# Four graph-attention layers in one program: the two dot-product layers take the weighted sums of two units together

## The reference

```python
h = jnp.maximum(_layernorm(x, axis=-1), 0.0)          # before each layer
# layer 0, one head; layer 1 the same with 4 heads, biases and a leaky relu on the scores
Q = jnp.matmul(x, W_q); K = jnp.matmul(x, W_k); V = jnp.matmul(x, W_v)
scores = jnp.einsum('bnd,bmd->bnm', Q, K) * scale
scores = jnp.where(adj == 0, NEG, scores)
attn = jax.nn.softmax(scores, axis=-1)
out = jnp.matmul(attn, V)
# layer 1: out = leaky_relu(mean over the 4 heads of prop_h @ v_h, 0.2)
```

## Time and profile before

| | us |
|---|---|
| median of 3 runs (lowest, highest) | 3523.88 (3518.64, 3524.6) |
| the profiled execution, its own time | 3535.45 |
| its span, first to last instruction | 3533.6 |
| first dot layer | about 30 to 255 |
| second dot layer | about 296 to 1232 |
| additive layer, not touched | 1232 to 3178 |
| last layer, not touched | 3178 to 3533 |

### The profile page before, as it was taken

How to read it: one execution, slowest core, us unless ns; L and a number is a source line. 1 busy time by engine, 2 the same in 40 slices (tenths; PEclk the granted TensorE clock), 3 DMA queues, 4 the chain that set the end, 5 groups by cost and what they waited for, 6 DMA issues and landing times. The chain is left out here.

```text
span 3533.6 us, 78782 instructions
## 1 busy us (share of the span) xinstructions
PE 3074.6 (87%) x30972; PEld 1704.5 (48%) x30972; DVE 3034.8 (86%) x4698; ACT 2898.4 (82%) x3774; POOL 992.2 (28%) x869
## 2 busy tenths in 40 slices
PE   7988998999999879898898998988988888878875
PEld 5765666666666633333343333333333333336664
DVE  7886887878888789999999999999999999965775
ACT  4546887778877769999999999999999999975665
POOL 4434666666666600000000000000000000005674
PEclk9998999999999989999999999999999999987897
DMA  7640000000000000000000000000000000002221
GB/s 246 222 139 16 20 21 20 23 18 24 21 21 19 13 11 10 10 10 10 10 10 10 10 10 10 10 10 10 10 10 10 10 10 10 10 5 67 57 63 30
DMA packets 68411, 111.58 MB, mean 32 GB/s; under 512 B 26452, under 2 KB 26582, under 8 KB 68054
## 3 DMA queue, kind: packets, MB, share of 16 engines
q1 hardware_dynamic: 68054, 106.69, 9.8%
HBM read 86.61 MB, written 18.87 MB: 30 GB/s over the span
## 5 line engine op out<-in xcount | busy, mean ns | idle before, releaser
L1120 ACT ACTIVATE l_scalar_ring<-l_w,l_r 128x1024 f32<-128x1024 f32 x1568 | 1650.0, 1148 | 34.4 <-DVE l_values L1171 27.7
L1236 DVE TENSOR_SCALAR l_vector_ring<-l_w_code,l_r_code 128x2048 f32<-128x2048 f32 x1264 | 1605.9, 1341 | 3.1 <-PE scores L1045 0.5
L1035 PE MATMUL scores<-l_scalar_ring,l_signs 128*32 128x512 f32 x6272 | 767.9, 608 | 130.2 <-ACT l_scalar_ring L1120 129.9
L1045 PE MATMUL scores<-l_vector_ring,l_signs_code 128*32 128x512 f16 x10112 | 685.0, 396 | 90.4 <-DVE l_vector_ring L1236 89.6
L462 POOL TENSOR_TENSOR l_masked<-l_relu,mask 128x512 f32<-128x512 f32 x512 | 585.9, 1166 | 344.2 <-ACT l_relu L664 322.9
L250 ACT COPY probs_t<-turned 128x512 f32<-128x512 f32 x576 | 324.7, 587 | 430.1 <-PE turned L209 429.7
L172 POOL TENSOR_TENSOR stat<-stat,minus_half 128x8 f32<-128x8 f32 x32 | 71.6, 2239 | 1931.1 <-DVE stat L167 1931.0
L1045 PEld LDWEIGHTS scores<-l_vector_ring,l_signs_code 128*32 128x32 bf16 x10112 | 257.9, 96 | 543.2 <-DVE l_vector_ring L1236 213.8
L209 PE MATMUL turned<-ident,l_probs 128*128 128x128 f32 x3072 | 438.1, 288 | 12.2 <-issue 7.6
L277 ACT ACTIVATE l_probs<-l_logits,negmax 128x1024 f32<-128x1024 f32 x384 | 442.9, 1153 | 7.0 <-DVE negmax L268 7.0
L1035 PEld LDWEIGHTS scores<-l_scalar_ring,l_signs 128*32 128x32 f32 x6272 | 192.2, 110 | 492.3 <-issue 255.9
(11 more groups left out here) (249 smaller groups left out, 2857.6 us busy)
## 6 DMA issues: line engine op xcount, KB each, us to landing
mask<-masks_kept SPq DMA_DIRECT2D x192, 256.0 KB, 2.7
l_adj<-adj SPq DMA_DIRECT2D x64, 512.0 KB, 5.9
masks_kept<-l_mask_ring SPq DMA_DIRECT2D x64, 256.0 KB, 4.9
x_res<-x SPq DMA_DIRECT2D x8, 256.0 KB, 4.8
out<-x_res SPq DMA_DIRECT2D x8, 256.0 KB, 2.9
l_h<-l_h SPq DMA_DIRECT2D x8, 128.0 KB, 2.8
l_kl<-l_dh SPq DMA_DIRECT2D x32, 2.0 KB, 1.9
l_kl<-l_dl SPq DMA_DIRECT2D x32, 2.0 KB, 1.8
```

Of the source, the lines that this page charges most:

```text
L1035: last = nc.tensor.matmul(s.scores[g * ROWS:(g + 1) * ROWS, buf, half, :], signs[:, window], scalar_ring[:, at % SCALAR_RING, g, halves[ha ...
L1045: last = nc.tensor.matmul(s.scores[g * ROWS:(g + 1) * ROWS, buf, half, :], signs_code[:, par, g % 2, window], parts(vector_ring[:, at % VE ...
L1120: last = nc.scalar.activation(scalar_ring[:, at % SCALAR_RING, g, :], w[:, par, :], ACT.Relu, bias=r[:, par, column:column + 1])
L1236: last = nc.vector.tensor_scalar(vector_ring[:, at % VECTOR_RING, g:g + 2, :], w_code[:, par, :, :], r_code[:, par, 0, column:column + 1], ...
```

## The change

Units are taken in pairs (2p, 2p+1). The turned probabilities of a unit go to one of four buffers `probs_t[:, n % 4]`. The product of pair p runs one pair later, half of it in iteration 2p+2 and half in 2p+3: each step has four blocks of 128, and for each the two units side by side, one in either half of `outT`. There is then one `copy_out` a pair and one turn of the output a pair (`turn_pair`, 128 columns against the weights `wv_pairs`, which hold the value weights of the two heads on their diagonal), two iterations after the product began. DVE does `copy_out` at the head of the even iteration, ahead of its half copy, and finishes both units of the pair behind that copy (`finish_pair`). The pipeline runs over the end of a graph without emptying. The first two graphs are written out ahead of the loop, so that the loop runs two times in place of three.

```diff
+            def turn_pair(q, p):
+                pe.wait_ge(sems["out_copied"], STARTS + q + 1)
+                wait(pe, sems["unit_done"], STARTS + 2 * q)
+                nc.tensor.matmul(pair_out, s.turned_out[:], wv_pairs[:, p % PAIRED, :], start=True, stop=True
+                                 ).then_inc(sems["out_turned"], 1)
+
+            def pair_times_values(par, q, p, step):
+                if step == 0:
+                    pe.wait_ge(sems["half0_copied"], STARTS + 2 * q + 2)
+                    pe.wait_ge(sems["half1_copied"], STARTS + 2 * q + 2)
+                    wait(pe, sems["out_copied"], STARTS + q)
+                    wait(pe, sems["unit_done"], STARTS + 2 * q)
+                for j in range(step * NB // 2, (step + 1) * NB // 2):
+                    for odd in range(2):
+                        last = nc.tensor.matmul(s.outT[odd * D:(odd + 1) * D, 0:P], values[:, par, j, :],
+                                                probs_t[:, p % 2 * 2 + odd, j, :], start=(j == 0), stop=(j == NB - 1),
+                                                skip_group_check=True)
+                if step == 1:
+                    last.then_inc(sems["out_ready"], 1)
...
                     turn_probs(pe, s, sems, probs[:, n % 2, :], u)
-                    if n > 0:
-                        turn_out(pe, s, sems, u - 1, 0, unit_out, weights=wv[:, (n - 1) % H, :])
+                    if n % 2 == 0 and not (first and p < 2):
+                        turn_pair(b * Q + p - 2, (p - 2) % Q)
...
-                    wait(pe, sems["unit_done"], STARTS + u)
-                    if n == 0:
+                    if n == 2:
                         pe.wait_ge(sems["values_ready"], b + 1)
-                    probs_times_values(pe, s, sems, values[:, par, :, :], u)
-                turn_out(pe, s, sems, b * U + U - 1, 0, unit_out, weights=wv[:, H - 1, :])
+                    if not (first and p < 1):
+                        pair_times_values(par if p else 1 - par, b * Q + p - 1, (p - 1) % Q, n % 2)
...
+            def finish_pair(b, p):
+                v.drain()
+                finish(b, 2 * p, b * U + 2 * p)
+                if leaky:
+                    v.drain()
+                finish(b, 2 * p + 1, b * U + 2 * p + 1)
...
-                    v.drain()
-                    copy_half(v, nc.vector.tensor_copy, s, sems, 0, u)
-                    if n > 0:
-                        finish(b, n - 1, u - 1)
+                    p = n // 2
+                    if n % 2 == 0 and not (first and p < 2):
+                        copy_out(v, s, sems, b * Q + p - 2)
+                    copy_half(v, nc.vector.tensor_copy, s, sems, 0, u, probs_t[:, n % 4, :, :])
+                    if n % 2 == 0 and not (first and p < 2):
+                        if p < 2:
+                            finish_pair(b - 1, p - 2 + Q)
+                        else:
+                            finish_pair(b, p - 2)
...
-                    copy_out(v, s, sems, u)
                     for k in fills_at(n, project):
                         take_fill(b + 1, 1 - par, k)
...
-            with v.Fori(0, B // 2 - 1) as t:
-                for par in range(2):
-                    graph(2 * t + par, par, True, False)
+            graph(0, 0, True, False, first=True)
+            graph(1, 1, True, False)
+            with v.Fori(0, (B - 4) // 2) as t:
+                for i in (2, 3):
+                    graph(2 * t + i, i % 2, True, False)
```

More of the change, by code:

```diff
@@ L243, in turn_out, with copy_half @@
                        start=True, stop=True).then_inc(sems["out_turned"], 1)
-def copy_half(eng, copy, s, sems, half, u):
+def copy_half(eng, copy, s, sems, half, u, to=None):
     eng.wait_ge(sems["turned_ready"], STARTS + u + 1)
     n = s.NB // 2
-    copy(s.probs_t[:, half * n:(half + 1) * n, :], s.turned[:, half * n:(half + 1) * n, :]
+    copy((s.probs_t if to is None else to)[:, half * n:(half + 1) * n, :], s.turned[:, half * n:(half + 1) * n, :]
          ).then_inc(sems[f"half{half}_copied"], 1)
@@ L321, in dot_layer @@
     CONST = float(D)
+    PAIRED = max(1, H // 2)
+    Q = U // 2
     with ExitStack() as ctx:
@@ L332, in dot_layer @@
         wT = sb("wT", [P, 2, H, R], F32)
+        wv_pairs = sb("wv_pairs", [P, PAIRED, P], F32)
+        probs_t = sb("probs_t", [P, 4, NB, P], F32)
+        rinv = sb("rinv", [P, 8], F32)
         bias_prod = sb("bias_prod", [P, H], F32)
@@ L636, in _ @@
                 score(0, 0, u, u)
-            with pe.Fori(0, B // 2 - 1) as t:
-                for par in range(2):
-                    graph(2 * t + par, par, True, False)
+            graph(0, 0, True, False, first=True)
+            graph(1, 1, True, False)
+            with pe.Fori(0, (B - 4) // 2) as t:
+                for i in (2, 3):
+                    graph(2 * t + i, i % 2, True, False)
             graph(B - 2, 0, True, False)
             graph(B - 1, 1, False, True)
+            turn_pair(B * Q - 2, Q - 2)
+            for step in range(2):
+                pair_times_values(1, B * Q - 1, Q - 1, step)
+            turn_pair(B * Q - 1, Q - 1)
         @block.scalar
@@ L669, in graph @@
                     u = b * U + n
-                    copy_half(a, nc.scalar.copy, s, sems, 1, u)
+                    copy_half(a, nc.scalar.copy, s, sems, 1, u, probs_t[:, n % 4, :, :])
                     if not (last_graph and n + 1 == U):
@@ L766, in finish @@
                 if h == 0:
[L767 removed]
+                    nc.vector.scalar_tensor_tensor(out=acc[:], in0=unit_out[:, 0:D], scalar=scale,
                                                    in1=v_bias[:], op0=ALU.mult, op1=ALU.add).then_inc(sems["unit_done"], 1)
                 else:
[L770 removed]
+                    nc.vector.scalar_tensor_tensor(out=acc[:], in0=unit_out[:, 0:D], scalar=scale,
                                                    in1=acc[:], op0=ALU.mult, op1=ALU.add).then_inc(sems["unit_done"], 1)
@@ L776, in finish, with graph @@
                     nc.vector.scalar_tensor_tensor(out=xb, in0=leaked[:], scalar=1.0 / H, in1=xb, op0=ALU.mult, op1=ALU.add)
-            def graph(b, par, project, last_graph):
+            def finish_pair(b, p):
[4 more added lines that the diff above has]
+                finish(b, 2 * p + 1, b * U + 2 * p + 1)
+            def graph(b, par, project, last_graph, first=False):
                 for n in range(U):
                     u = b * U + n
-                    v.drain()
-                    copy_half(v, nc.vector.tensor_copy, s, sems, 0, u)
-                    if n > 0:
-                        finish(b, n - 1, u - 1)
+                    p = n // 2
+                    if n % 2 == 0 and not (first and p < 2):
[6 more added lines that the diff above has]
+                            finish_pair(b, p - 2)
                     if not last_graph or n + 2 < U:
@@ L800, in graph @@
                         take_values(b + 1, 1 - par)
-                v.drain()
-                finish(b, U - 1, b * U + U - 1)
             nc.vector.memset(one[:], 1.0)
@@ L818, in _ @@
             nc.vector.tensor_scalar(up[:], s.ident[:], UP, None, ALU.mult)
+            nc.vector.memset(wv_pairs[:], 0.0)
+            v.drain()
             v.wait_ge(sems["weights_in"], 16 * WEIGHT_LOADS)
+            for odd in range(2):
+                rows = slice(odd * D, (odd + 1) * D)
+                nc.vector.tensor_copy(wv_pairs[rows, :, rows], wv[rows, min(odd, H - 1):H:2, :])
             hold_waits(v, sems)
@@ L884, in _ @@
                 v.wait_ge(sems["x_in"], 16 * (B - 2))
-            with v.Fori(0, B // 2 - 1) as t:
-                for par in range(2):
-                    graph(2 * t + par, par, True, False)
+            graph(0, 0, True, False, first=True)
+            graph(1, 1, True, False)
+            with v.Fori(0, (B - 4) // 2) as t:
+                for i in (2, 3):
+                    graph(2 * t + i, i % 2, True, False)
             graph(B - 2, 0, True, False)
             graph(B - 1, 1, False, True)
+            for p in (Q - 2, Q - 1):
+                copy_out(v, s, sems, B * Q + p - Q)
+                finish_pair(B - 1, p)
 def elu_parts(v, s, sems, z, low, high):
```

16 lines of the change are left out of this document (7 added, 9 removed).

## The result

| | before | after |
|---|---|---|
| median of 4 runs each, us | 3521.26 | 3554.06 |
| lowest, highest | 3517.07, 3524.6 | 3549.39, 3566.64 |
| the profiled execution, its own time | 3535.45 | 3553.77 |

The ratio is 1.0099, 95% interval 1.007 to 1.0128: the change makes the kernel slower by about 33 us. The forecast was +21.

The account below looks back on a forecast made before the run. The prediction took PE to bound both dot layers. Its terms, second-layer graphs +30, loop -6, first layer -4, set-up +1, sum to +21 us on the median 3523.9, forecasting 3545, range 3497 to 3592.

Parts of the forecast that it names:

- The working of the even unit: Second layer, behind a fill: after T, `copy_out` at 1.80, turn-out 2.14, product 3.49, next turn 4.52 us.
- The price of a pair: Second layer, pairs with a fill: 4.52 + 3.30 = 7.82 us against 7.24, +0.58, ten a graph in seven graphs.
- I count +0.1 each: Second layer, even units 2 and 4, behind fills that turn `y`: `copy_out` half a microsecond sooner, +0.1 us each.
- The end of a graph: -1.7: Second layer, last unit of a graph: no wait for its own output, 3.1 us in place of 4.77.
- One fewer: -6: Loop turning once instead of twice: each turn costs 3.8 us of idle PE plus about 2 at half clock.
- The first layer, -4: First dot layer: shorter odd units and graph ends against longer even units, -0.6 us a graph, -4 for seven.
- The two products saved at the start are paid at the end. 0: Start and end of each layer: two products saved, then paid, net 0 us.
- +1 for the set-up: Start of each layer: four small DVE steps set up `wv_pairs`, +0.5 us a layer, +1 together.
- The clock falls: Rival, chance 0.11: PE's idle 1.2 us bring half-speed matmuls in half of 70 even units, +52 us, 3597.
- The fill copy does not hold the turn-out: Rival, chance 0.21: `copy_out` ready by T + 0.93, even unit 3.64, pair 6.94 us; total -42, 3482.
- The third rival: Chance 0.11: stall a third as long, +0.2 us a pair, paid by graph ends and the loop; 3524.
- the prediction's second working of the even unit: PE's own queue: 2.09, plus 1.21 late turn-out, 0.1 width, 0.19 weights not loaded ahead; product at 3.59 us at most.

Follow-up runs that it names:

- the kernel with this part alone: Kernel before, with only two graphs of each dot layer written out ahead of the loop on PE and DVE; 3526.53 us, ratio 0.9996.
- the kernel of before with two moves: Kernel before, units singly; in the second layer DVE's fill copy moved behind the next finish, the leak behind the logits; 3658.01 us, ratio 1.0384.

## Why the prediction was right, and where it was off

- **The mechanism was right.** `copy_out` behind the fill copy makes PE's turn-out, and all that is queued behind it, wait 1.00. The working of the even unit holds to 0.06 us at each step.
- **The price of a pair came out, in part by luck.** The ten pairs from unit 4 to unit 23 of an ordinary graph take 72.8 us in the trace of before and 78.6 after: +0.58 a pair, as forecast (79.4 to 79.7 in the three graphs with fills that stand outside the loop). But the units are not 4.52 and 3.30 but 4.47, 4.18, 3.75 and 3.34 in turn. The kernel with the leak behind the logits shows the forecast's own pattern (4.47 and 3.34) and takes 77.6: the forecast stall alone is worth +0.48 a pair, and the slow L809 adds the rest.
- **"I count +0.1 each"** for the units 2 and 4 was mis-sized. The first four units of a graph take 15.27 before and 16.32 after: +1.05. Most of it is unit 2, 4.09 for 3.31. The prediction lets `copy_out` come half a microsecond sooner there, 1.3 after T, and so it does (1.29). But the turn-out then comes at 1.63 and not at 0.93, which its own working would have priced at 0.7. Unit 0 adds 0.4, unit 1 gives 0.2 back; unit 3 takes 4.7 in both kernels.
- **"The end of a graph: -1.7"** measured -1.4 over the last eight units (28.00 to 26.63). With the two above, an ordinary graph (116.06 before, 121.55 after) costs 5.5 and not 4.3. Over seven graphs, with one that differs by 6.4, that is +39 for +30. This is the largest error.
- **"One fewer: -6"** was mis-sized: what remains after these terms for the graphs around the loop is -3. The two turns of before cost 5.8 and 4.4 in the units on either side. The one that is left costs 6.9, since DVE's own stop at the turn now makes PE stand a second time (the rows at 786.51 to 793.57), with matmuls at 1.2 GHz behind it. The trace of the kernel with this part alone shows -2.7 in the layer; its timed runs don't resolve it.
- **The first layer, -4:** from its first turn to its last finish it gains 0.9. The prediction's own terms add up to -0.93 a graph and not the -0.6 that it states. Measured are -3.1 over the second to the seventh graph, -0.5 each, and -2.9 for the first, where two products are saved. The last graph, which has no fill, was put at nothing and costs 1.8: its even units take 3.56, and one 4.44, in place of about 3.1 to 3.3. The two products paid at the end cost 3.3. So the -4.2 between first and last turn in the table agrees with the forecast by luck.
- **"The two products saved at the start are paid at the end. 0", and +1 for the set-up:** in the second layer the first graph gives 3.6 back (its difference is +1.9, not 5.5), and the end, from the last turn to the last step of DVE, is 3.1 longer: they nearly cancel, as forecast. The set-ups are +1.2 and +0.3.
- **The sum:** seven graphs +39.4, loop -3.1, first layer -0.9, set-ups +1.5, start and end of the second layer -0.9 (with -0.4 for its last graph), the untouched additive layer +0.5. Together that is +36 in the trace, +33 by the medians, +21 forecast.
- **"The clock falls" did not happen in the pairs.** PE stood for about 1.0 us or less in 80 places, and the granted clock of the layer is 1.00. It was lower once, behind the wait of 3.00 at the turn of the loop, and in the kernel of before with two moves, whose waits are up to 2.2, it is 0.93. **"The fill copy does not hold the turn-out"** fell too, though its remark that a longer unit gives ACT a lead is what happens behind every slow L809. The third rival, that gains and losses cancel, is excluded by the interval. The wide turn-out needed no more than the 0.65 taken: its finish stands at 719.62, 0.64 behind it. The two finishes of 0.28 in 0.66 show that the written drain costs what the earlier trace rows show (0.38 from start to start). In the prediction's second working of the even unit, by PE's own queue, the 0.36 between turn-out and scores was read at a place at 1.2 GHz; in after it is 0.33 at full clock.

What I missed is that the change moved the block's last DVE steps into the time in which POOL adds masks. The trace of before has rows for it: here the leak takes 0.51 in place of 0.23, until 0.1 behind the end of POOL's second addition.

```profile
530.82 2.27 POOL L462 TENSOR_TENSOR l_masked<-l_relu,mask 128x512 f32<-128x512 f32 x2 [0.81 <-ACT l_relu L664]
...
532.66 0.51 DVE L774 SCALAR_TENSOR_TENSOR l_leaked<-l_acc 128x64 f32<-128x64 f32 x1
```

I priced these steps at what they took at their old place.

## What to carry to other kernels

An instruction that waits late for another engine is cheap only at a place in its queue where nothing urgent stands behind it. When it delays step A, don't take A out of its way alone: look who stands next (here the half copy and the finishes), for the stall moves there and nearly half the loss stays. And price a moved DVE step by what POOL runs at the new place, not by its duration at the old one.

## What the runs showed of the hardware

- **POOL holds some DVE steps until its running instruction ends.** A 128x64 step that takes 0.22 to 0.23 alone took 1.08 (two inputs from SBUF), 1.05 (one input, multiplied by a constant, SBUF to SBUF) or 1.15 (the leak, which reads `l_acc` twice) beside POOL's additions. A reduction took 0.22 at the same place. Copies of 512 columns from PSUM (0.66 to 0.69 over the layer), finishes with one input from PSUM (0.28 to 0.29) and logits (1.27 to 1.29) showed nothing of it. The Trainium skill, "GPSIMD Engine Reference", 1. Specifications, says that GpSimd shares its SBUF interfaces with VectorE, and names as those that collide the VectorE instructions in a 2-port mode and those with two SBUF inputs; "SBUF — State Buffer", SBUF: two separate sides, adds that the one that comes first keeps them for its whole instruction. By the rows with two inputs and by the reduction, the trace agrees. That the step with one input ran in a 2-port mode would fit, but no row shows the mode.
- **The same code at two clocks.** The last layer, untouched, took 359.1 us at a granted clock of 0.80 in one execution and 340.9 at 0.86 in the other, more than half of the effect under study. With one profile of each kernel, compare stretches rather than spans.
